# Gathering each tile of edges once, into rings of 72 slots read through registers, in three of the four edge loops of a graph network

## The reference

```python
h = relu(layernorm(x)); x = x + L0(h)   # 8-head attention over edges, batch norms, feed-forward
h = relu(layernorm(x)); x = x + L1(h)   # sum over edges of (h W)[src] * filter(edge_attr_32, edge_weight)
h = relu(layernorm(x)); x = x + L2(h)   # 1-head attention, logit = leaky(s[src] + edge_attr_128 . v)
h = relu(layernorm(x)); x = x + L3(h)   # normalized sum over edges, relu
# in each: msg = table[src] * weight ; out = segment_sum(msg, dst)
```

## Time and profile before

| | us |
|---|---|
| median of 3 runs | 4847.12 |
| lowest and highest | 4845.93, 4855.51 |
| span of the profiled execution | 4836.7 |
| PE busy in it | 3551.4 (73%) |
| DVE busy | 3365.7 (70%) |
| POOL busy | 3211.3 (66%) |
| ACT busy | 2021.2 (42%) |

### The profile page before, as it was taken

How to read it: one execution, slowest core, us unless ns; L and a number is a source line. 1 busy time by engine, 2 the same in 40 slices (tenths; PEclk the granted TensorE clock), 3 DMA queues, 4 the chain that set the end, 5 groups by cost and what they waited for, 6 DMA issues and landing times. The chain is left out here.

```text
span 4836.7 us, 67940 instructions
## 1 busy us (share of the span) xinstructions
PE 3551.4 (73%) x13730; PEld 2548.5 (53%) x13730; DVE 3365.7 (70%) x9609; ACT 2021.2 (42%) x5849; POOL 3211.3 (66%) x3433
## 2 busy tenths in 40 slices
PE   8888777787798677767666578888888555555555
PEld 5566555565654455555555355555555444444444
DVE  7799999999833677777777477777777444444444
ACT  2466666666543433333333466666666000000000
POOL 1477777777200377777777577777777577777776
PEclk9866777867899878888888677777777677777777
DMA  3254454445300444444443244444443233333333
GB/s 118 89 139 136 138 139 138 139 138 139 90 16 3 119 122 127 125 125 125 126 125 108 80 111 113 114 114 114 114 114 109 80 111 112 112 112 112 111 112 100
DMA packets 346051, 540.75 MB, mean 112 GB/s; under 512 B 75816, under 2 KB 237899, under 8 KB 345675
## 3 DMA queue, kind: packets, MB, share of 16 engines
q0 software_dynamic: 146432, 386.15, 28.6%
q1 hardware_dynamic: 191755, 142.86, 10.3%
q10 hardware_dynamic: 7488, 7.72, 0.5%
HBM read 506.37 MB, written 30.07 MB: 111 GB/s over the span
## 5 line engine op out<-in xcount | busy, mean ns | idle before, releaser
L747 POOL DMA_INDIRECT e_rows<-table,src_idx x2496 | 2360.7, 946 | 1079.0 <-issue 538.8
L811 DVE TENSOR_TENSOR acc<-acc,banks 128x273 f32 (+3 forms) x3328 | 1298.9, 390 | 819.4 <-PE banks L799 646.0
L799 PE MATMUL banks<-e_rows,e_hot 128*128 128x128 f32 (+1 forms) x3328 | 990.0, 440 | 705.9 <-DMA e_rows<-table,src_idx 442.6
L799 PEld LDWEIGHTS banks<-e_rows,e_hot 128*128 128x128 f32 x3328 | 754.6, 256 | 935.1 <-DMA e_rows<-table,src_idx 484.6
L747 POOL DMA_INDIRECT edge_rows<-table,src_idx x832 | 800.5, 962 | 256.1 <-issue 188.5
L799 PE MATMUL banks<-edge_rows,e_hot 128*128 128x273 f32 x1664 | 728.3, 569 | 13.2 <-DVE edge_rows L1259 12.3
L799 PE MATMUL banks<-e_rows,e_weighted_hot 128*128 128x257 f32 x1664 | 645.5, 520 | 16.5 <-ACT e_weighted_hot L962 16.0
L926 ACT ACTIVATE e_apart<-const,dst_loc 128x128 bf16<-128x128 f32 x1664 | 505.9, 388 | 15.4 <-PEq L527 9.1
L799 PEld LDWEIGHTS banks<-edge_rows,e_hot 128*128 128x128 f32 x1664 | 385.9, 264 | 104.5 <-DVE acc L811 19.2
L799 PEld LDWEIGHTS banks<-e_rows,e_weighted_hot 128*128 128x128 f32 x1664 | 366.3, 249 | 108.3 <-issue 29.0
L962 ACT ACTIVATE e_weighted_hot<-e_hot,e_weight 128x128 f32<-128x128 f32 x832 | 254.3, 388 | 9.8 <-issue 1.1
(11 more groups left out here) (314 smaller groups left out, 4961.4 us busy)
## 6 DMA issues: line engine op xcount, KB each, us to landing
e_edge_in<-in_edge_attr SPq DMA_DIRECT2D x832, 80.0 KB
e_rows<-table,src_idx POOLq DMA_INDIRECT x2496
e_node_rows<-node_line SPq DMA_DIRECT2D x104, 256.0 KB, 3.4
edge_rows<-table,src_idx POOLq DMA_INDIRECT x832
table<-n_row SPq DMA_DIRECT2D x49, 132.0 KB, 1.7
table<-fn_row ACTq DMA_DIRECT2D x49, 129.0 KB
X<-in_x SPq DMA_DIRECT2D x1, 6272.0 KB
values<-table SPq DMA_DIRECT2D x49, 128.0 KB, 2.0
```

What stands on the lines that cost most here:

```text
L747: nc.gpsimd.indirect_dma_start(out=rows[:, u, q, 0:width], out_offset=None, in_=table, in_offset=bass.IndirectOffsetOnAxis(ap=at, axis=0)) ...
L799: nc.tensor.matmul(banks[:, 2 + q % turn, 0:width], onehot, rows, start=True, stop=True).then_inc(summed_tile, 1)
L811: nc.vector.tensor_tensor(at, at, banks[:, 2 + q % turn, 0:width], ALU.add).then_inc(added, 1)
```

## The change

- The blocks are worked on in their natural order, rotated: the order begins at the block whose first tile lies furthest ahead of an even spread (`size_key` is now that lead, `begin` the block, its tile and its step). Given that start, a fixed rule bounds which tile a step can need (`newest`), so that waits can be written as constants.
- e1, e2 and e3 fetch each tile once, in 98 batches of 8 (`FETCHES`, 784 gathers for a loop) and into a ring of 72 slots (`HELD`). Gather g waits for the sum of step g - 24 (`last_use(g - 72)` = g - 72 + 48). A step finds its rows by a slot number that PE reads into registers, 8 words for each batch (`load_slots`).
- Work on gathered tiles in e1 (filters, edge attributes, logit products) goes by fetched tile: 98 times, not 104. In batches 19, 35, 52, 69, 86 and 103 no new batch of tiles is needed (`fresh`).
- In e2 `value` adds the row's word to `edge_q` once for each fetched batch, and then takes the logit of each of the 8 steps by itself, with an instruction of one column whose input address comes from a register; DVE reads 8 more words for each batch (`fetch_places`), and 10 in place of 12 block words.
- To make room, `X` leaves SBUF behind the layer-0 tail: the node rows go to DRAM (`nodes`), and e1 and e2 load and store them through a ring of 5 (`NodeRing`, 131 KB each way for a block; on ACT's queue in e1 and SP's in e2). e3 loads all of them at its start (`gc_x`). Several other tiles are laid into parts of `acc`.
- The preparation transposes the sources, and the first stage the cutoffs, tile by tile (7 PE transposes each), and stores them twice in a row in DRAM, to be read from the first tile on; 11 small POOL instructions make the tables of slots and places. `pick_cutoff` and the splitting of the cutoffs into three parts are gone. POOL clears the part of `acc` that e1 used as scratch.
- e0 keeps its ring of 4 batches and its 832 gathers.

```diff
+def newest(s):
+    at = min(s, WORK - 1)
+    ranks = -(-NB * (at + 1) // WORK) - 1
+    return at if ranks == 0 else at - ranks + 1
+def needed(j):
+    return newest(j * G + G - 1) // G
+def fresh(j):
+    if j >= BATCHES or j > 0 and needed(j) == needed(j - 1):
+        return None
+    return needed(j)
+def last_use(g):
+    return min(g + NB - 1, WORK - 1)
...
-                    now = step(v.scalar_tensor_tensor(size_key[:, :], length[:, :], 64.0, block_of[:, 0:NB], ALU.mult, ALU.add))
+                    now = step(v.scalar_tensor_tensor(size_key[:, :], first_tile[:, 0:NB], 64.0 * NB, prep_("lead_of"), ALU.mult, ALU.add))
...
+                    for g in range(GROUPS):
+                        last = nc.tensor.transpose(banks[:, 4 + g // 4, g % 4 * P:(g % 4 + 1) * P], end_f[:, 1, g, :], ident)
+                    last.then_inc(src_turned, 1)
...
                         each(ROWS_OUT, sp, NB, store)
+                        sp.wait_ge(cut_tiles_ready, 1)
+                        keep_twice(cutoff_line, cut_tiles)
+                        sp.wait_ge(tiles_out, 64)
...
+        def fetch_tiles(pool, table, width, rows, fetched, summed_tile, spare_read=()):
+            for g in range(FETCH_W):
+                if g == SPARE:
+                    for read, count in spare_read:
+                        pool.wait_ge(read, count)
+                if g >= HELD:
+                    pool.wait_ge(summed_tile, summed(0, last_use(g - HELD)))
+                nc.gpsimd.indirect_dma_start(out=rows[:, g % HELD, 0:width], out_offset=None, in_=table,
+                                             in_offset=bass.IndirectOffsetOnAxis(ap=src_fetch[:, g:g + 1], axis=0)).then_inc(fetched[g // G % FETCH_RING], 16)
...
+        def load_slots(j):
+            return nc.values_load_multi_w_load_instructions(
+                slot_line[:, bass.ds(j * G, G)], engines=[PE_ENGINE], min_val=0, max_val=HELD - 1,
...
+                if self.with_fetch and inside(n + 2):
+                    self.fetch_at = fetch_places(n + 2)
...
-                                v.tensor_tensor(sums[:, 0, :].unsqueeze(2), rows[:, u, :, D + 1:D + 2], edge_q[:, bass.ds(n * G, G)].unsqueeze(2), ALU.add).then_inc(logit_ready, 1)
-                                dve.wait_ge(logit_ready, n + 1)
-                                v.scalar_tensor_tensor(val[:, :], sums[:, 0, :], slope, sums[:, 0, :], ALU.mult, ALU.max).then_inc(val_ready, 1)
+                            m = fresh(n)
+                            if m is not None:
+                                dve.wait_ge(gathered[m % FETCH_RING], landed(m, FETCH_RING))
+                                logits = edge_q[:, m * G:(m + 1) * G]
+                                slots = rows[:, m % FETCH_RING * G:(m % FETCH_RING + 1) * G, D + 1:D + 2].squeeze(2)
+                                v.tensor_tensor(logits, slots, logits, ALU.add).then_inc(logit_ready, 1)
+                                dve.wait_ge(logit_ready, m + 1)
+                            for q in range(G):
+                                logit = edge_q[:, bass.ds(fetch_at[q], 1)]
+                                last = v.scalar_tensor_tensor(val[:, q:q + 1], logit, slope, logit, ALU.mult, ALU.max)
+                            last.then_inc(val_ready, 1)
...
-        ahead = RowAhead(G if many else ROW_REGS)
+        ahead = RowAhead(G if many else G + 2, not many)
...
-                            sum_tile(pe, j, q, hot[:, u % 2, q, :], rows[:, u, q, :], summed_tile, added, width, sum_banks)
+                            row = rows[:, bass.ds(slots[q], 1), :].squeeze(1)
+                            sum_tile(pe, j, q, hot[:, u % 2, q, :], row, summed_tile, added, width, sum_banks)
...
+        class NodeRing:
+            def load(self, queue, start, k):
+                if k >= NB:
+                    return
+                if k >= X_RING:
+                    queue.wait_ge(self.x_out[k % X_RING], 16 * (k // X_RING))
+                b = load_ranked(SP_ENGINE if queue is nc.sync else ACT_ENGINE, k)
+                start(self.at(k), node_rows(nodes, b)).then_inc(self.x_in[k % X_RING], 16)
+            def wait(self, dve, k):
+                dve.wait_ge(self.x_in[k % X_RING], 16 * (k // X_RING + 1))
+            def store(self, start, k, b):
+                start(node_rows(nodes, b), self.at(k)).then_inc(self.x_out[k % X_RING], 16)
```

More of the change, by code:

```diff
@@ L39 @@
 STEPS = (BATCHES + 4) * G
+WORK = TILES + NB - 1
+FETCHED = TILES + 1
+FETCHES = -(-FETCHED // G)
+FETCH_W = FETCHES * G
+TWICE = TILES + FETCH_W
+HELD = 72
+X_RING = 5
+X_AHEAD = X_RING - 1
+FETCH_RING = HELD // G
+SPARE = HELD - 2 * G
 HALF = STEPS // 2
+HIDDEN_BLOCKS = 14
 SLOTS = G * P
@@ L606, in _ @@
                             last.then_inc(product, 1)
+                            if b == 44:
+                                pe.wait_ge(cut_steps, 6)
+                                for g in range(GROUPS):
+                                    last = nc.tensor.transpose(banks[:, 6 + g // 4, g % 4 * P:(g % 4 + 1) * P], cut[:, g, :], ident)
+                                last.then_inc(cut_turned, 1)
                     @blk.vector
@@ L752, in gather_batches @@
                 pool.wait_ge(gathered[u], 16 * G * TURNS)
+        def fetch_tiles(pool, table, width, rows, fetched, summed_tile, spare_read=()):
[7 more added lines that the diff above has]
+                                             in_offset=bass.IndirectOffsetOnAxis(ap=src_fetch[:, g:g + 1], axis=0)).then_inc(fetched[g // G % FETCH_RING], 16)
+            for n in range(FETCHES - FETCH_RING, FETCHES):
+                pool.wait_ge(fetched[n % FETCH_RING], landed(n, FETCH_RING))
+        def load_slots(j):
+            return nc.values_load_multi_w_load_instructions(
+                slot_line[:, bass.ds(j * G, G)], engines=[PE_ENGINE], min_val=0, max_val=HELD - 1,
+                skip_runtime_bounds_check_because="cut to the ring's size when they were made")[1]
         def arrived(n, u):
@@ L847, in softmax_edges @@
                 node = node_work(st) if node_work else None
-                gathered = [sem(f"{tag}_gathered{u}") for u in range(RING)]
+                gathered = [sem(f"{tag}_gathered{u}") for u in range(RING if many else FETCH_RING)]
                 restart_in = [sem(f"{tag}_restart_in{u}") for u in range(2)]
@@ L1072, in sums_of @@
                                     pe.wait_ge(weighted, 2 * j + q // (G // 2) + 1)
[L1073 removed]
+                                by, row = hot[:, u, q, :], rows[:, u, q, 0:sum_w]
                             else:
                                 pe.wait_ge(weighted, j * G + q + 1)
[L1076 to L1085 removed]
+                                by, row = weighted_hot[:, u % 2, q, :], rows[:, bass.ds(slots[q], 1), 0:sum_w].squeeze(1)
+                            sum_tile(pe, j, q, by, row, summed_tile, added, sum_w)
                         if many:
[L1088 removed]
                             dst_side(0, load_blocks(PE_ENGINE, 0), 0, G)
@@ L1302, in _ @@
                             keep_dst(1)
-                        value(1, 1)
+                        value(1, 1, None if many else fetch_places(1))
                         if many:
@@ L1351, in batch @@
                             if still:
-                                value(j + 2, (r + 2) % RING)
+                                value(j + 2, (r + 2) % RING, None if many else ahead.fetch_at)
                             if last is not None and not even:
@@ L1487, in batch @@
                         def batch(j, r, k=None, last=None):
[L1488 to L1489 removed]
+                            two = fresh(j + 2)
+                            if filtered and two is not None:
+                                scale_radial(two, two % RING, two % 2)
                             if filtered and r % 2 == 0:
@@ L1501, in batch @@
                                 node.act_keep(act, k)
-                            if filtered and inside(j + 2):
-                                keep_scaledT(j + 2, r % 2)
+                            if filtered and two is not None:
+                                keep_scaledT(two, two % 2)
                         if filtered:
@@ L1570, in batch @@
                             odd = filtered and k is not None and u % 2 == 1
-                            sums_of(j, u, 0)
+                            one, two, slots = fresh(j + 1), fresh(j + 2), load_slots(j)
+                            sums_of(j, u, 0, slots)
                             if even and last is not None:
@@ L1682, in batch @@
                                 node.dve_row(dve, last)
-                            if filtered and inside(j + 1):
-                                filter_rows(j + 1, un, 0)
+                            if filtered and one is not None:
+                                filter_rows(one, 0)
                             add(3)
@@ L1687, in batch @@
                                 node.dve_aggregate(dve, k)
```

(8 more changed lines are left out.)

412 lines of the change are left out of this document (257 added, 155 removed).

## The result

The changed kernel takes 4905.25 us (median, 4903.67 to 4906.74) against 4848.57 of the kernel before: 1.0118 of its time, 95% interval 1.0104 to 1.0133. That is 57 us slower; 35 us faster were forecast, and the time lies 10 us above the range. The profiled execution's span is 4902.1 us, 65.4 more than before.

What follows compares the result with a forecast made beforehand. POOL's gathers were taken to bound e1 and e3, POOL and DVE nearly at once e2. Start, e1, e2, e3: +9 - 48.5 + 59 - 54 = -34.5 us, giving span 4802, median 4813; range 4745 to 4895.

Steps and rivals of the forecast that it cites:

- What bounds the kernel: Loops e1 to e3: POOL's gathers set e1 and e3, POOL and DVE nearly together e2; e1 -48.5, e3 -54 us.
- the last sums stand behind the last gather: End of e3: one more batch of sums, 8 sums and a one-hot, behind the last gather, about +6.2 us.
- Start: Preparation, first stage and tail stages before e1: transposes, small POOL instructions, cutoffs' stores and node stores, sum +9 us.
- e2, value: DVE in e2: one add and eight one-column instructions at 0.13, 1.24 us for 0.39, +0.85 for each batch.
- e2, registers: DVE in e2: reads of 10 and 8 words, 0.58 + 0.50 = 1.08 us, +0.41 for each batch, bounds 0 and +0.67.
- e2, absorbed: DVE in e2: a third of its 0.61 us waits for PE credited, -0.20 for each batch, bounds -0.61 and 0.
- sign of being wrong: e2: prediction wrong if PE falls behind and DVE's waits for it grow instead of shrinking.
- Eight split logits and the second read are dear: Rival, e2: nothing absorbed, pace 11.2 us or more, e2 +125 or more, total about 4880; chance 0.22.
- its decisive pace: That rival's threshold in e2: it decides from 10.99 us for a batch, where e2's +103 is reached.
- e1 not following: Rival, e1: PE's slot reads and later DVE adds keep the pace at 10, total 4861 us; chance 0.11.
- the 10.4 us between span and median: Whole run: profiled span of 4836.7 us lies 10.4 below the median of runs; difference taken as unchanged.

Runs made afterwards that it cites:

- e3: Not a run: a gather loop of the kernel; from its first gather to end of span 1055.9 us before the change, 1003.0 after.
- e0: Not a run: a gather loop of the kernel, left with 832 gathers; PE busy 879 us of 1103 there in the kernel before.
- window: Changed kernel, logits kept twice and picked through one register address and a zero-one table, one read of 12 words: 4770.07 us, 0.9864 of the kernel before.
- read_twice_8: Kernel before, e2 reading a batch's 8 block numbers a second time and using them: 5612.30 us against 5609.57; repeated, 1.0030 of the kernel before.
- first_partition: Changed kernel, places copied to partition 0 of another tile and read there: 5684.74 us against 5609.57 of the kernel before; repeated, 5841.47 against 5687.30.
- twelve_words: Changed kernel, first read taking all 12 words of the row instead of 10: 4881.61 us.
- read_moved: Changed kernel, second read (8 places) moved from behind add(6) to behind add(0): 4883.14 us.
- one_read: Changed kernel, one read of 18 words (10 block words and 8 places side by side) replacing two: 4995.69 us, 1.0315 of the kernel before.
- one_word: Changed kernel, second read taking one word instead of 8, all eight logits using that register: 4820.49 us.
- read_twice_1: Kernel before, e2 reading one word, the block of add(7), a second time and using it: 5623.81 us against 5609.57.

## Why the prediction was wrong

- **What bounds the kernel**: right for e1 and e3. 48 gathers fewer gave -49.5 and -52.9 us with their ends, within 1.1 us of the forecast (whose terms for e1 add up to -48.8), and the last sums stand behind the last gather as said: e3's two last batches merge to one group of PE that begins 2.9 us behind the last gather and runs 10.1 us.

```profile
4883.14 10.13 PE L941 MATMUL banks<-e_rows,e_hot 128*128 x30 [3.23 <-DMA e_rows<-table,src_fetch]
```

- **Start**: +6.7 for +9; right within its bounds.
- **e2, value**: 1.36 us for the forecast 1.24, +12 us. The 8 x 0.13 = 1.04 measured 1.05, by luck: it holds with addresses from registers, while with fixed columns eight instructions follow at 0.07. The 0.12 that was missing stands ahead of them, behind the add. The 0.07 is near the 0.061 of the Trainium skill ("VectorE: DVE Perf Modes", the section on the TRN2 errata). By that page alone the forecast would have been 4756 us, an estimate, since register addresses aren't in it; and instructions that need one another's result follow at some 0.2 us in window's timeline, not at 0.07.
- **e2, registers: the step that failed.** "a read is some 0.17 + 0.041 for each word; ... +0.41 (bounds 0 ... and +0.67)." It measured 2.38 - 1.10 = +1.28, above the upper bound, 0.87 x 104 = 90 us more than forecast. The cost of a read was taken from idle gaps, and a gap is what the running add leaves of a read. In the earlier trace rows the read begins 0.03 us behind the start of `add(6)`, so most of the add's 0.42 us hides a part of it, and 0.67 of idle time is left of a read recorded with 0.85. A second read has nothing to hide behind and costs its whole length. (The line also took the 0.21 that stands between two adds without any read for a part of the reads; without that slip it gives +0.27, still further off.) The +1.28 consists of +0.62 for a second read of 8 words (read_twice_8), +0.44 for the change of partition (first_partition) and +0.21 for 10 words instead of 12 (twelve_words). The first of the three stood in the trace of the kernel before, as e0's read of 8 words with 0.60 us; the other two did not. All pitches together, each with the recorded length of its reads in the same batches (18 aligned: in the four odd ones among them); "other partition" means that each read follows one from another partition:

| reads | recorded, us | pitch, us | pitch less reads (unrounded) |
|---|---|---|---|
| 12 words, aligned | 0.85 | 1.10 | 0.25 |
| 10 aligned | 1.07 | 1.31 | 0.25 |
| 18, begin aligned | 1.57 | 1.81 | 0.25 |
| 18, begin 8 bytes off | 4.06 | 4.31 | 0.25 |
| 10, other partition (read_moved) | 1.29 | 1.54 | 0.25 |
| 12 + 1, same partition | 0.85 + 0.31 | 1.43 | 0.28 |
| 12 + 8, same partition | 0.85 + 0.60 | 1.72 | 0.28 |
| 10 + 8, same partition | 1.07 + 0.59 | 1.94 | 0.28 |
| 10 + 8, 8 bytes off | 1.07 + 1.84 | 3.19 | 0.28 |
| 10 + 1, other partition | 1.29 + 0.53 | 2.10 | 0.28 |
| 12 + 8, other partition | 1.07 + 0.81 | 2.16 | 0.28 |
| 10 + 8, other partition | 1.29 + 0.81 | 2.38 | 0.28 |

So the pitch is the reads and a fixed rest, 0.25 us with one read and 0.28 with two; without a read it is 0.63. The lengths follow a rule to 0.04 us, which is mine, fitted to this table: 0.09 for a read, 0.25 for each group of 4 words (counted from the read's first) that begins at a multiple of 16 bytes, 0.22 for each word besides, and 0.22 if the read before went to another partition. It says how the cost goes, not what in the hardware does it. The Trainium skill ("Runtime: NRT & Kernel Launch", section "Instruction fetch mechanics") gives a register load some 200 ns for each register, and the page has HBM as the source. These words lie in SBUF; where they are not aligned they cost nearly that (18 words in 4.06 us), where they are, far less (12 in 0.85). By this page the 18 words of the changed kernel would be 3.6 us for 2.4 of the 12 before, +1.2 for each batch, an estimate that comes near +1.28 by luck, since the recorded lengths are 2.10 and 0.85.
- **e2, absorbed**: -0.20, and 9.50 + 0.97 + 1.28 = 11.75 against a measured (1241.4 - 40.9)/104 = 11.54: -0.21. The size is right, the 0.61 it was taken from is not: 23.0 of the 39.7 us were DVE's own register reads, and 0.39 for each batch could be absorbed. The forecast's sign of being wrong, that DVE's waits for PE grow, came by the profile's label alone (39.7 to 103.7); without the reads they fell from 16.7 to 4.5. Nor is it a rule: in window nothing was absorbed.
- **The rivals**: "Eight split logits and the second read are dear" (0.22) is what happened, by the read and not by the split; its decisive pace was 10.99, measured 11.54. e1 not following: out, its gathers run at 1.251 us to the end. The sum with the measured terms is -34.5 + 90 + 12 = +68, against +65.4 in the span. In the medians it is +57, because the forecast took the 10.4 us between span and median as unchanged; they were 3.2.

## What to carry to other kernels

Idle time behind a register read is charged in this profile to whatever semaphore came last; if it repeats to a hundredth of a microsecond while real waits scatter, it is the queue's own work. Ask for the line of the read: its length is recorded, and only the first read behind an instruction is partly hidden. Count register reads as work of the engine that reads: by aligned groups of four words, with all words in one partition, and padded rather than cut (12 words cost less than 10). Before a loop gets fewer instructions on one engine, ask what the other engines need in return: 48 gathers fewer were worth up to 60 us, and where eight elements were picked by register the loop grew by 161, since its engine had only 0.5 us to spare in each batch.

## What the runs showed of the hardware

- A read of words of SBUF into registers stops DVE's queue, 0.31 us for one word, 0.60 for 8, 0.85 for 12, 1.07 for 10 and 1.57 for 18; two reads in a row add up.
- When the words began 8 bytes off a multiple of 16 (from the tile's start), 18 words took 4.06 us instead of 1.57, 10 words 2.30 instead of 1.07 (e1 of one_read), and 8 words 1.84 instead of 0.59.
- A read that follows one from another partition took 0.22 us more: 1.29 against 1.07 for 10 words, 0.81 against 0.59 for 8, 0.53 (one_word) against 0.31 (read_twice_1) for one. A pair that goes back and forth between partitions 0 and 96 costs 0.44 (2.38 against 1.94).
- Addresses from registers: eight instructions of one column in 0.57 us with fixed addresses, 1.05 with eight register addresses, 0.56 when all eight use one register.
